# An mLSTM layer with a ternary-weight FFN on one core: the opening as explicit lists of calls, new weight passes, decays on ScalarE, masks on GpSimd, and filler matmuls

## The reference

```python
log_D = fg_mat + ig[..., None, :]            # masked to s >= t, else -inf
D = jnp.exp(log_D - max_log_D)
qk = jnp.einsum('bnsd,bntd->bnst', qh, kh) / jnp.sqrt(jnp.float32(DH))
C = qk * D
normalizer = jnp.maximum(jnp.abs(C.sum(-1, keepdims=True)), jnp.exp(-max_log_D))
h = jnp.einsum('bnst,bntd->bnsd', C / (normalizer + EPS_BACKEND), vh)
# per head: hn = (h - mean) * rsqrt(var + eps) * outnorm_weight;  x = x + hn
...
def _weight_quant(w):
    scale = 1.0 / jnp.clip(jnp.mean(jnp.abs(w)), 1e-05)
    wq = jnp.clip(jnp.round(w * scale), -1.0, 1.0) / scale
def _act_quant(x):
    scale = 127.0 / jnp.clip(jnp.max(jnp.abs(x), axis=-1, keepdims=True), 1e-05)
    xq = jnp.clip(jnp.round(x * scale), -128.0, 127.0) / scale
...
gate = jax.nn.silu(_bitlinear(x, w_gate)); up = _bitlinear(x, w_up)
return _bitlinear(gate * up, w_down)         # added to x
```

## Time and profile before

| | us |
|---|---|
| median of 3 runs | 661.33 (661.14 to 661.69) |
| the profiled execution | 657.75 |
| its span, first to last instruction | 655.9 |
| TensorE, VectorE, ScalarE, GpSimd busy | 567.0, 541.9, 476.4, 295.2 |

### The profile page before, as it was taken

One profiled execution on the slowest core, in us unless ns is written; L12 is line 12 of the kernel. 1 busy time (PEld: TensorE's weight loads), 2 busy tenths in 40 slices (PEclk: granted clock), 3 DMA queues, 4 the chain that ended last, 5 costly groups with the idle time before them and its releaser, 6 DMA issues. The chain is left out here.

```text
span 655.9 us, 12646 instructions
## 1 busy us (share of the span) xinstructions
PE 567.0 (86%) x3566; PEld 365.2 (56%) x3566; DVE 541.9 (83%) x1442; ACT 476.4 (73%) x716; POOL 295.2 (45%) x475
## 2 busy tenths in 40 slices
PE   1825557799999999999999999999999998899995
PEld 0824444376566665576647656666557664455442
DVE  3149777998989898989899898989898889988763
ACT  1878776587858796788768785879678876855653
POOL 2012436544664546463564466454646346334200
PEclk9999999999999999999999999999999999999999
DMA  8944724101234102620252123410171041000001
GB/s 330 376 137 159 273 91 147 47 2 49 82 94 165 49 18 74 218 77 0 81 176 80 48 81 116 140 48 30 64 219 55 0 161 48 33 17 12 22 17 48
DMA packets 34208, 63.74 MB, mean 97 GB/s; under 512 B 2688, under 2 KB 19200, under 8 KB 31616
## 3 DMA queue, kind: packets, MB, share of 16 engines
q1 hardware_dynamic: 33600, 62.92, 28.0%
q10 hardware_dynamic: 576, 0.44, 0.3%
HBM read 54.84 MB, written 8.52 MB: 97 GB/s over the span
## 5 line engine op out<-in xcount | busy, mean ns | idle before, releaser
L573 PE MATMUL GU<-WQ,xqT 128*128 128x512 bf16 x1024 | 239.4, 381 | 6.6 <-DVE FF L1184 6.5
L573 PEld LDWEIGHTS GU<-WQ,xqT 128*128 128x128 bf16 x1024 | 97.2, 98 | 109.0 <-issue 6.5
L603 PE MATMUL ACC<-WQ,FF 128*128 128x512 bf16 x512 | 115.8, 379 | 2.9 <-ACT FF L829 2.9
L810 ACT ACTIVATE FF<-GU,cgu 128x512 f32<-128x512 f32 x128 | 86.7, 690 | 21.0 <-PE GU L573 19.3
L1184 DVE TENSOR_TENSOR FF<-FF,GU 128x512 f32<-128x512 f32 x128 | 85.1, 680 | 15.3 <-ACT FF L810 12.3
L603 PEld LDWEIGHTS ACC<-WQ,FF 128*128 128x128 bf16 x512 | 49.4, 98 | 59.3 <-ACT FF L829 3.7
L818 ACT ACTIVATE FF<-FF,magic,hs 128x1024 f32<-128x1024 f32 x64 | 79.2, 1242 | 3.1 <-DVE hs L1215 3.1
L776 ACT ACTIVATE work<-AT,pb 128x128 f32<-128x128 f32 x128 | 48.1, 455 | 15.8 <-POOL pb L1480 15.3
L520 PE MATMUL AT<-vext,CT 128*128 128x129 f32 x256 | 51.7, 295 | 4.7 <-ACT gate_parts L714 3.8
L1500 POOL TENSOR_TENSOR work<-work,norm_bc 128x512 f32<-128x512 f32 x32 | 41.8, 1306 | 23.8 <-ACT work L776 23.8
L1466 POOL TENSOR_SCALAR pb<-den 128x4 f32<-128x4 f32 x32 | 7.0, 218 | 98.7 <-DVE den L1122 98.7
(11 more groups left out here) (117 smaller groups left out, 1201.4 us busy)
## 6 DMA issues: line engine op xcount, KB each, us to landing
bc<-gate_rows SPq DMA_DIRECT2D x32, 512.0 KB, 6.4
xin<-in_x SPq DMA_DIRECT2D x32, 256.0 KB, 2.8
kT<-in_ctx_t SPq DMA_DIRECT2D x8, 1024.0 KB, 4.8
vext<-in_ctx SPq DMA_DIRECT2D x32, 256.0 KB, 3.5
out<-FF SPq DMA_DIRECT2D x32, 256.0 KB, 2.3
WQ<-in_w_gate SPq DMA_DIRECT2D x4, 1024.0 KB, 13.0
FF<-in_w_up SPq DMA_DIRECT2D x4, 1024.0 KB, 15.5
FF<-in_w_down SPq DMA_DIRECT2D x4, 1024.0 KB, 4.7
```

Source lines behind the costliest of these rows:

```text
L573: last = nc.tensor.matmul(dst, xqT[:, b, P * k:P * (k + 1)], w[:, k, 512 * j:512 * (j + 1)], start=(k == 0), stop=(k == KC - 1))
L603: last = nc.tensor.matmul(ACC[:, :], hT[:, b % 2, P * k:P * (k + 1)], WD[:, k, :], start=(k == 0), stop=(k == JT - 1))
L810: nc.scalar.activation(sg[:, j % 2, :], GU[:, 2 * (j % 2), :], ACT.Silu, scale=cgu[:, b, 0:1]).then_inc(silu_done, 1)
```

## The change

It leaves the list of `iteration` for the loop and the end nearly as it was, and replaces the unrolled iterations -1, 0 and 1 by a function `opening()` on each engine, with its own lists of bank users (`OPENING_TP`, `OPENING_AT`).

- The weights: `weight_divide` is gone from ScalarE. `weight_lift` (multiply by the factor, add the large constant) runs on GpSimd for ten quarters and on VectorE for the two quarters (0, 0) and (0, 1). The last pass is `weight_clip` on VectorE for the gate matrix (two instructions a quarter, as before) and `weight_sign` on ScalarE for the eight quarters of the other two: one `Sign` of the lifted value minus the constant. The sums write into `xqT`, no longer into `GU`. Semaphores count by quarter, and a quarter of `w_down` is loaded as soon as the quarter in its place is used up.
- The decays: `decay_argument` and the mask tile are gone. `exp_decay` is four Exp instructions, one per head, with the bias from `cols`. `mask_scores` on GpSimd sets the scores above the diagonal to zero, and `weigh` also caps the decay at 1.
- The start: VectorE waits for one constant and not for three; two memsets go from VectorE to GpSimd.
- TensorE: `keep_warm(n)` issues n matmuls of ones by ones, 135 in all, between the calls ahead of the first `gate_up`.

```diff
+        def staged(m, c):
...
+            if m == 0:
+                return early[:, 2048 * c:2048 * (c + 1)]
+            if m == 2 and c < 2:
+                return early[:, 2048 * (2 + c):2048 * (3 + c)]
+            c = c if m == 1 else c - 2
+            return FF[:, 2048 * c:2048 * (c + 1)]
...
-            def load_quarter(m, src, c):
+            def load_quarter(m, c):
...
                 if m == 2:
-                    sp.wait_ge(w_ready, 4 + c + 1)
+                    sp.wait_ge(w_done[2 + c], 1)
...
                 if step_of(g) == 0 and b == 0 and j == 0:
-                    pe.wait_ge(w_ready, 8)
-                    pe.wait_ge(wsum, 12)
+                    pe.wait_ge(wsum[2], 4)
+                    for i in range(8):
+                        pe.wait_ge(w_done[i], 1)
...
+            def keep_warm(n):
...
+                for _ in range(n):
+                    nc.tensor.matmul(GU[:, 3, 0:P], ones[:, :], ones[:, :], start=True, stop=True)
...
-                act.wait_ge(arg_done, g * 4 + (b + 1))
-                nc.scalar.activation(CT[:, NH * b:NH * (b + 1), :], CT[:, NH * b:NH * (b + 1), :], ACT.Exp,
-                                     scale=-1.0).then_inc(exp_done, 1)
+                act.wait_ge(cols_ready, cols_at)
+                act.wait_ge(bc_in[b], bc_in_at)
...
+                for k in range(NH):
+                    r = NH * b + k
+                    last = nc.scalar.activation(CT[:, r, :], bc[:, r, 0, :], ACT.Exp, bias=cols[:, 0, r:r + 1], scale=-1.0)
+                last.then_inc(exp_done, 1)
...
-            def weight_divide(m, c):
+            def weight_sign(m, c):
...
+                act.wait_ge(w_lifted[4 * m + c], 1)
...
+                nc.scalar.activation(WQ[:, m, 2048 * c:2048 * (c + 1)], lifted(m, c), ACT.Sign,
+                                     bias=magic[:, 1:2]).then_inc(w_done[4 * m + c], 1)
...
-                V.tensor_tensor(CT[:, r, :], CT[:, r, :], scores[:, b, :].rearrange("p (h s) -> p h s", h=NH),
-                                ALU.mult).then_inc(ct_ready, 1)
+                V.scalar_tensor_tensor(CT[:, r, :], CT[:, r, :], 1.0, scores[:, b, :].rearrange("p (h s) -> p h s", h=NH),
+                                       ALU.min, ALU.mult).then_inc(ct_ready, 1)
...
-            dve.wait_ge(const_in, 16 * 3)
+            dve.wait_ge(gate_w_in, 16)
...
+            def mask_scores(g, b):
...
+                pool.wait_ge(sc_ready, sc_ready_at)
...
+                G.affine_select(out=scores[:, b, :], in_=scores[:, b, :], compare_op=ALU.is_ge, fill=0.0, base=0,
+                                pattern=[[0, NH], [1, P]], channel_multiplier=-1).then_inc(sc_masked, 1)
...
+            def weight_lift(m, c):
...
+                pool.wait_ge(w_scaled, m + 1)
+                if m == 2 and c < 2:
+                    pool.wait_ge(w_done[6 + c], 1)
+                G.tensor_scalar(lifted(m, c), staged(m, c), w_factor[:, m:m + 1], MAGIC, ALU.mult, ALU.add).then_inc(w_lifted[4 * m + c], 1)
```

More of the change, by code:

```diff
@@ L407, in iteration, with opening @@
                 store(former, 0)
-            for it in range(-1, FULL):
-                iteration(it)
+            def opening():
+                load_x(0, 0)
+                load_x(0, 1)
+                load_x(0, 2)
+                load_x(0, 3)
+                load_quarter(0, 0)
+                load_k(0)
+                load_quarter(0, 1)
+                load_quarter(0, 2)
+                load_quarter(0, 3)
+                load_x(1, 0)
+                load_x(1, 1)
+                load_v(0, 0)
+                load_quarter(1, 2)
+                load_quarter(1, 1)
+                load_quarter(1, 0)
+                load_x(1, 2)
+                spread_rows(0, 0)
+                spread_rows(0, 1)
+                load_quarter(1, 3)
+                load_x(1, 3)
+                spread_rows(0, 2)
+                load_v(0, 1)
+                load_x(2, 0)
+                load_v(0, 2)
+                spread_rows(0, 3)
+                load_quarter(2, 1)
+                load_quarter(2, 0)
+                load_x(2, 1)
+                load_quarter(2, 2)
+                load_quarter(2, 3)
+                load_x(2, 2)
+                load_k(1)
+                load_x(2, 3)
+                load_v(0, 3)
+                load_k(2)
+                spread_rows(1, 0)
+                load_v(1, 0)
+                spread_rows(1, 1)
+                spread_rows(1, 2)
+                load_v(1, 1)
+                spread_rows(1, 3)
+                load_v(1, 2)
+                load_v(1, 3)
+                store(0, 0)
+            opening()
             with sp.Fori(FULL, FULL_END) as it:
@@ L600, in down @@
                 if step_of(g) == 0 and b == 0:
-                    pe.wait_ge(w_ready, 12)
+                    for i in range(8, 12):
+                        pe.wait_ge(w_done[i], 1)
                 for k in range(JT):
@@ L962, in _ @@
+            act.dma_start(CT[:, 0, 0:3 * KC * 8], gate_w).then_inc(gate_w_in, 16)
+            act.dma_start(bias_col[:, :], gate_b).then_inc(gate_b_in, 16)
+            act.dma_start(norm_bc[:, :], norm_w.rearrange("h d -> (h d)").partition_broadcast(P)).then_inc(norm_w_in, 16)
             act.wait_ge(dve_const, 1)
-            for it in range(-1, FULL):
-                iteration(it)
+            opening()
             with act.Fori(FULL, FULL_END) as it:
@@ L1399, in _ @@
                 dve.sem_inc(o_out[r], 16)
-            dve.wait_ge(pool_const, 1)
-            for it in range(-1, FULL):
-                iteration(it)
+            opening()
             with dve.Fori(FULL, FULL_END) as it:
```

666 lines of the change are left out of this document (503 added, 163 removed), and 10 rows, old and new, of tables (OPENING_AT, OPENING_TP).

## The result

| | before | after |
|---|---|---|
| median, us | 661.51 (661.14 to 661.82) | 673.72 (672.92 to 683.24) |
| ratio, 95% interval | | 1.0181 [1.0161, 1.0201] |
| profiled execution, us | 657.75 | 672.92 |
| span, us | 655.9 | 671.2 |
| first `gate_up`, us | 105.30 | 81.83 |

The 683.24 is a disturbed execution, which the ratio leaves out. The spans differ by 15.3 us: -10.2 at the transpose of the gates of group 2, +21.5 in the five periods from there to the gates of group 7, and +4.0 behind them. (The loop's first transpose lies between the first two of these marks and is 8.7 us earlier than before.) I had forecast 647.5 from -18.5 at the loop's start and +4.7 in the loop.

The account below looks back on a forecast made before the run. TensorE was taken to bound the loop but not the opening, where ScalarE carries the way. Opening -18.5 plus loop +4.7 gives -13.8, so 661.3 becomes 647.5 us; range 637 to 660, with 641 to 655 at 62 in 100.

Parts of the forecast that it names:

- -18.5 at the loop's start: Opening: the shorter way to the third `gate_up`, less work moved behind it, starts the loop at 183.5 against 202.0.
- +4.7 in the loop: Loop: five iterations, each with +0.95 us of new TensorE wait; bounds 0 and +7.
- I price that at nothing: Loop: 16 fewer VectorE instructions gain nothing, since VectorE waits 0.95 us for a `silu` there and had time in hand.
- GpSimd has the room: Loop: four mask passes of 0.6 to 1.2 us fit on GpSimd, busy for 38.5 of 70 us.
- 5.7 us an iteration: Loop: VectorE's freed time, cited for the rival that the loop absorbs the decays (637 to 640, 12 in 100).
- The wait for the copy of scores: Loop's head: two sequences' longer Exp work on ScalarE delays the copy, +0.95 us of TensorE wait.
- first `head_scale`: Opening: GpSimd gets its first `head_scale` at 43.5 us, after gate rows, broadcast, Exp and four short calls.
- third `gate_up`: Opening: starts about 1 us after the first `silu`, at 91 against 112.6, -21.6 us.
- my 83.0: Opening: TensorE's work in us from the third `gate_up` to the loop, including calls moved there.
- my 9.5: Opening: TensorE's idle us from third `gate_up` to loop, 5.5 around the gates and rows of group 1, 4 elsewhere.
- The first (slow lifts): Rival, opening: a lift costs the upper bound of 5.3 us, eight add 22.4, result 669.9; 9 in 100.
- The second: Rival, opening: late calls in the explicit lists, fillers among them, hold engines and lose 8 to 10 us; 656; 15 in 100.

Follow-up runs that it names:

- e7: Kernel before with one 16x1 copy (0.13 us) on VectorE ahead of the scan of the running maximum; 681.4 us (1.029).
- e5: Changed kernel with 24 do-nothing VectorE instructions, and GpSimd's residual of (former, 1) held behind VectorE's `x_norm`; 659.9 us (0.989).
- e6: Kernel before with GpSimd's residual held behind VectorE's `x_norm`; 657.9 us (0.994).
- e12: Kernel before with the new decays and masks, 12 do-nothing VectorE instructions, and GpSimd's residual held behind `x_norm`; 666.1 us (1.004).
- e1: Changed kernel with 24 do-nothing instructions added to VectorE ahead of its first scale of the weights; 675.2 us (1.017).
- e9: Changed kernel with only GpSimd's residual held behind VectorE's `x_norm`, no instructions added on VectorE; 665.3 us (1.004).
- e3: Changed kernel with `decay_argument`, one Exp and the mask tile back as before, weights and opening as changed; 665.4 us (1.004).
- e15: Changed kernel with the decays and masks of before from group 2 on and 24 do-nothing VectorE instructions, without GpSimd's added wait; 653.0 us (0.986).
- e13: Changed kernel with decays and masks of before from group 2 on, 24 do-nothing VectorE instructions, GpSimd's residual held behind `x_norm`; 646.8 us (0.976).

## Why the prediction was wrong

- **The loop: the step that failed.** "VectorE loses 16 instructions of 0.356 us ... I price that at nothing", the masks likewise because "GpSimd has the room", and bounds of 0 and +7 for five iterations. It was +21.5. I looked for covers by who waits for whom, and never asked which two engines work at the same instant. VectorE's list between jump and `copy_hT` has no reserve, and its pace hangs on which of two unconnected instructions starts first, by less than 0.1 us. e7 shows the mechanism alone, in the kernel before; e5 and e6 take it away. VectorE's freed time gave nothing, as assumed: over four periods it is busy for 12.1 us less in e12 than in e6, and idle for 18.6 more. (It was never 5.7 us an iteration: the 16 instructions overlap, and 23.6 us in five iterations is 4.7.) The stretch from 130 to 200 us, by which I called the loop TensorE's, lies ahead of the loop; TensorE is busy for 96% of the five periods before, so that reading happens to hold.
- **The terms I did price there were about right.** The wait for the copy of scores is +0.78 for my +0.95; four Exp take 1.28 us together for 1.33. With nothing colliding the new decays cost 0.2 to 2.6 us an iteration, 1.3 on average (e12 against e6), near my +0.95.
- **The code fetch was in no term.** It gave half of VectorE's loss in the changed kernel (2.17 of 4.05) and reached TensorE as the waits for the gates. Its removal alone (e1) freed 6.3 us of idle time on TensorE, and 5.2 of them were lost again to slower matmuls, mostly behind the waits for the copy; with the collision gone it costs 9.0 us in the loop (e9 against e5).
- **The opening: right in mechanism, too large.** Gate rows at 33.5 (forecast 32.7); first `head_scale` 47.2 (43.5, the first miss: 3.7 us); a lift is 1.97 us (2.5), yet the last ends at 87.8 (85); first `silu` 93.7 (90); third `gate_up` 96.6 (91); from there 96.7 us to the loop (92.5). That is -8.7 for -18.5: 5.6 lost ahead of the third `gate_up` and 4.2 behind it. Ahead of it one part was misread in the rows: I put the third `gate_up` 1 us behind the first `silu`, but it already was 4.0 behind it before (108.58 and 112.62), and is 2.9 now. TensorE also ran partly at the lower level (0.84 granted between 50 and 105 us), a term I did not have. Behind the third `gate_up` TensorE is busy for 86.0 of the 96.7 us and idle for 10.7: the work was 3.0 more than my 83.0, the waits 1.2 more than my 9.5. So the waits around the gates of group 1, where GpSimd had nothing for 16.9 us until 119.5, came to about what I had set down. What delayed the first `head_scale` no experiment took apart; it stays open.
- **Rivals.** The first (slow lifts) is refuted by 1.97 us. The second had the size of the opening's loss right: 8.7 instead of 18.5 would have given 657, for its 656; the rest is the loop. No rival had a loss of the loop in it, and none of my 9% for slower was for the right reason.
- **The decays help the opening and hurt the loop.** e3 against the changed kernel: gates of group 2 at 160.7 against 151.8; e3 against e15: 665.4 against 653.0; e13 keeps one and drops the other. The new opening, with its decays, is worth about 11 us: e13 against e6.

## What to carry to other kernels

When a change moves a tuned loop by tenths of a microsecond, look for pairs of long GpSimd passes and short chained VectorE instructions that start close together, and order them with a wait instead of leaving it to chance; a wait on an engine with slack can be worth more than work taken from the busy one. Look at the idle of each engine at the loop's jump and at the packets of the instruction queue before explaining a longer period by data. And price an operation by place: the same exchange gained in the opening and lost in the loop.

## What the runs showed of the hardware

- **A pass on GpSimd can hold a VectorE instruction until it ends, and 0.05 us decide.** The scan of 16x128 takes 0.47 us alone and 1.31 to 1.59 beside the residual's first pass; a sum of 16x128 0.28 against 1.18 to 1.35; `x_norm` 0.53 against 1.32. The traces of all 17 kernels have 57 scans that start within 0.4 us of the residual's first pass. Those that started at least 0.054 us ahead took 0.47, and it was then the residual that took longer (1.32 to 1.49 instead of 1.27). Those that started 0.050 us ahead or later ended 0.27 to 0.28 us after the residual's pass. There is nothing in between. The Trainium skill (GPSIMD Engine Reference, Specifications) says that GpSimd shares its interfaces to SBUF with VectorE, and meets VectorE instructions of two SBUF inputs or of a 2-port mode: scan and sum have two inputs, so the traces agree.
- **A loop's jump costs nothing or 1.9 to 2.3 us, by the place of the loop in the code.** The trace has 287 VectorE records from jump to jump in the changed kernel and 306 before; 24 instructions ahead of the loop removed the stall, 56 created it, with 20 or 21 more packets of 8 KB in q14 for four jumps. The Trainium skill (Runtime: NRT & Kernel Launch, Instruction fetch mechanics) says that a taken branch to code outside the two pieces held must be fetched first; the stall agrees. It gives 16 KiB for a piece, where the packets here have 8 KB; how much is held at a time no run shows.
- **TensorE's clock can fall behind a wait of 2.7 us, and need not.** In e1 each of the loop's four waits for the copy (2.69 to 2.70 us) was followed by some 3 us at the lower of the two levels (1.2 against 2.4 GHz): in the iteration shown eight transposes took 1.03 instead of 0.61 us, and the granted clock of these four periods is 0.96 to 0.98, where the kernel before has 1.00. The changed kernel has four such waits of 2.80 to 2.84 us, and only the first brought it (a pair of matmuls 0.64 us, otherwise 0.39):

```profile
238.98 0.62 PE L659 MATMUL TPB<-ident,FF 128*128 128x128 bf16 x8 [2.84 <-DVE FF L1492]
239.48 0.66 PE L590 MATMUL AT<-vext,CT 128*128 128x129 f32 x2
239.94 0.64 PE L592 MATMUL AT<-state,qw 128*128 128x129 f32 x2
```

That period is 76.9 us long, the next, with the same wait, 75.2. In e7 three of four waits of 2.69 to 2.70 us brought it. So the length of the wait alone doesn't decide it here.
